# A four-layer graph network on one core: the relation layers as tiles of one relation each, edges ranked by relation on the chip

## What is computed

```
def _rgcn_layer(x, src, dst, edge_type, w_rel, root, bias):
    seg = dst * NUM_REL + edge_type
    sums = segment_sum(x[src], seg, N * NUM_REL)
    cnt = segment_sum(ones, seg, N * NUM_REL)
    mean = (sums / maximum(cnt, 1)[:, None]).reshape(N, NUM_REL, -1)
    return einsum('nrd,rdo->no', mean, w_rel) + x @ root + bias

edge_type = argmax(msg[:, 16:-16], axis=1)
h = relu(_rgcn_layer(x, src, dst, edge_type, w_rel1, root1, b1))
out = _rgcn_layer(h, src, dst, edge_type, w_rel2, root2, b2)
```

## Time and profile before

| | |
|---|---|
| median of 3 runs | 2677.25 us (2674.11 to 2680.0) |
| profiled execution, its own time | 2694.78 us |
| its span, first to last instruction | 2693.0 us |
| mean granted TensorE clock | 0.924 of 2.4 GHz |
| busy: PE, DVE, POOL, ACT | 2202.6, 2105.2, 1565.0, 1469.3 us |
| DMA | 376.34 MB, mean 140 GB/s |

### The profile page before, as it was taken

How to read it: one execution, slowest core, us unless ns; L and a number is a source line. 1 busy time by engine, 2 the same in 40 slices (tenths; PEclk the granted TensorE clock), 3 DMA queues, 4 the chain that set the end, 5 groups by cost and what they waited for, 6 DMA issues and landing times. The chain is left out here.

```text
span 2693.0 us, 53316 instructions
## 1 busy us (share of the span) xinstructions
PE 2202.6 (82%) x12829; PEld 1706.9 (63%) x12829; DVE 2105.2 (78%) x7193; ACT 1469.3 (55%) x4919; POOL 1565.0 (58%) x1653
## 2 busy tenths in 40 slices
PE   2998888888667776998776998567679999899996
PEld 2886667667555555886664898456646666555553
DVE  3667998899757776886897786588868888688886
ACT  0575555556556665665444777388844444333332
POOL 2778888888444435664886876333334444255554
PEclk9999999999878787999998989688889999899998
DMA  4666666666533435554675554344332223211221
GB/s 87 215 220 210 208 203 202 209 203 207 144 130 129 134 115 156 170 166 142 203 218 174 165 172 154 108 126 135 123 120 80 80 81 85 69 48 55 57 58 31
DMA packets 291561, 376.34 MB, mean 140 GB/s; under 512 B 59002, under 2 KB 142896, under 8 KB 291258
## 3 DMA queue, kind: packets, MB, share of 16 engines
q1 hardware_dynamic: 265658, 321.84, 37.6%
q0 software_dynamic: 25600, 51.09, 7.4%
HBM read 167.38 MB, written 206.80 MB: 139 GB/s over the span
## 5 line engine op out<-in xcount | busy, mean ns | idle before, releaser
L1808 PE MATMUL phase_p_w<-phase_w_rel,phase_rowsT 128*128 128x512 f32 (+1 forms) x1200 | 511.1, 528 | 10.3 <-ACT phase_rowsT L1861 10.2
L1889 DVE SCALAR_TENSOR_TENSOR phase_added<-phase_p_w,relation,phase_added 128x128 f32<-128x128 f32 x1200 | 349.9, 340 | 22.9 <-PE phase_p_w L1808 21.2
L1084 PE MATMUL phase_p_sum<-phase_whole,phase_link 128*128 128x128 f32 (+2 forms) x792 | 199.6, 338 | 146.7 <-ACT phase_whole L1201 65.3
L324 ACT ACTIVATE phase_sq<-phase_y 128x512 f32<-128x512 f32 x294 | 186.2, 634 | 229.9 <-POOL phase_y L457 178.9
L773 POOL DMA_INDIRECT phase_rows<-X,src_row x200 | 191.4, 957 | 202.0 <-PE phase_p_T L1816 168.0
L384 PE MATMUL phase_p_h<-W2c,phase_g 128*128 128x128 f32 x1568 | 231.5, 310 | 86.6 <-DVE phase_h L439 71.9
L384 PEld LDWEIGHTS phase_p_h<-W2c,phase_g 128*128 128x128 f32 x1568 | 220.3, 224 | 93.7 <-issue 77.1
L773 POOL DMA_INDIRECT phase_rows<-H,src_row x200 | 192.7, 963 | 135.0 <-PE phase_p_T L1816 108.8
L1152 POOL TENSOR_TENSOR phase_message<-R,scores 128x128 f32<-128x128 f32 x200 | 92.6, 464 | 284.3 <-PE phase_p_sum L1084 282.0
L1084 PEld LDWEIGHTS phase_p_sum<-phase_whole,phase_link 128*128 128x128 f32 x792 | 135.1, 213 | 188.2 <-ACT phase_whole L1201 87.8
L1808 PEld LDWEIGHTS phase_p_w<-phase_w_rel,phase_rowsT 128*128 128x128 f32 x1200 | 189.6, 193 | 86.6 <-issue 41.1
(11 more groups left out here) (254 smaller groups left out, 6876.6 us busy)
## 6 DMA issues: line engine op xcount, KB each, us to landing
H<-phase_h SPq DMA_DIRECT2D x196, 256.0 KB, 2.8
X<-phase_x SPq DMA_DIRECT2D x196, 256.0 KB, 2.3
phase_same<-same_keys SPq DMA_DIRECT2D x175, 256.0 KB
phase_xT<-in_x_columns SPq DMA_DIRECT2D x98, 256.0 KB, 4.0
Z<-phase_x SPq DMA_DIRECT2D x98, 256.0 KB
phase_x<-X SPq DMA_DIRECT2D x98, 256.0 KB
out<-phase_o SPq DMA_DIRECT2D x98, 256.0 KB
H<-R SPq DMA_DIRECT2D x50, 256.0 KB, 2.4
```

Source lines behind the costliest of these rows:

```text
L324: act.activation(self.buf(dst, g)[:, :, :], self.buf(src, g)[:, :, :], ACT.Square).then_inc(self.S[dst], 1)
L1084: last = nc.tensor.matmul(p[:, 0:width], loads.link(t), whole[1 - v][:, 0:width], start=False, stop=True)
L1808: nc.tensor.matmul(p_w[(PARTS * (t % UNROLL) + n) % BANKS][:, 0:b - a, :], rowsT[v][:, :], w[:, a:b, :], start=True, stop=True).then_inc(s ...
L1889: nc.vector.scalar_tensor_tensor(out=added[v][r % 2][:, :], in0=p_w[(PARTS * (t % UNROLL) + n) % BANKS][:, r % RG, :], scalar=plane(D["rel ...
```

## The change

An edge's rows are multiplied by the weight of its own relation alone. For that, edges are ranked by relation in `prepare_edges`: counts by relation and tile from two products with a triangle and with ones, a running sum over tiles, and starts of relations rounded up to whole tiles of 128. That gives each edge a place in a second order of 108 tiles (`REL_TILES`), each with edges of one relation only, and each tile the column of its weight (`weight_column`).

- `attention_rows` writes, by 100 indirect scatters of one number a slot, the source row of each edge to its place (`sorted_rows` in HBM); `hidden_rows` loads the list.
- A new stage `relation_products` gathers source rows in the relation order (ring of 12), transposes, multiplies each tile by one weight of 128 columns, and stores the products to HBM. Transposes, products and copies go in groups of four tiles. TensorE reads the column of the weight from SBUF into a register for each tile.
- `relation_rows` gathers the products in the order of targets (`sorted_read`), and sums. The factor 1/count (`share`, one reduction at the end of `gat_messages`) is multiplied into the table of equal keys, four tiles at a time. The root product stays in SBUF (`D["R"]`), so `x_root` goes. The bias is added to `Y` in `relation_products`, four tiles at a time, by DVE in place of POOL.
- Dense work is dealt anew: 70, 75, 55, 32 and 25 slots beside `hidden_rows`, `output_rows`, `gat_messages`, `weights_of_edges` and `gat_rows`, 70 beside the first `relation_products`, and the rest, 82, beside the first `relation_rows`. The output layer's two stages have none.

```diff
+REL_TILES = 108
+HIDDEN_SLOTS, OUTPUT_SLOTS, GAT_SLOTS, GAT_ROWS_SLOTS, PRODUCT_SLOTS = 70, 75, 55, 25, 70
...
 def prepare_edges(nc, io, W, D):
...
+                for n in range(2):
+                    part = D["relation"][:, n * T // 2:(n + 1) * T // 2, :].rearrange("p t r -> p (t r)")
+                    nc.tensor.matmul(p_here[:, n, 0:HALF], upto[:, :], part, start=True, stop=True)
+                    nc.tensor.matmul(p_tile[:, n, 0:HALF], ones[:, :], part, start=True, stop=True).then_inc(s["counted"], 1)
...
+                chained(nc.vector.tensor_tensor(D["relation"][:, :, :], D["relation"][:, :, :], wide(valid), ALU.mult))
+                nc.vector.memset(keep[:, :, :], 1.0).then_inc(s["relation_full"], 1)
...
+                chained(nc.vector.tensor_tensor_scan(flat(through), flat(keep), flat(in_tile), 0.0, ALU.mult, ALU.add))
...
+                chained(nc.vector.tensor_tensor(score[:, :, :], score[:, :, :], D["relation"][:, :, :], ALU.mult))
+                chained(nc.vector.tensor_reduce(place[:, :], score[:, :, :], AX.X, ALU.add))
+                chained(nc.vector.tensor_copy(D["sorted_read"][:, :], place[:, :]))
...
+                chained(nc.vector.tensor_tensor(D["sorted_write"][:, :], place[:, :], off[:, :], ALU.add))
...
+                chained(nc.vector.tensor_scalar(D["weight_column"][:, :], tile_f[:, :], float(RELATIONS - 1), float(F), ALU.min, ALU.mult))
...
 def attention_rows(nc, io, W, D, beside):
...
                         weighted(pool, nc, D, message, HEADS, s, t)
+                        moves.free(pool, t)
+                        pool.indirect_dma_start(out=io["sorted_rows"], out_offset=bass.IndirectOffsetOnAxis(ap=column(D["sorted_write"], t), axis=0),
+                                                in_=column(D["src_row"], t), in_offset=None, bounds_check=REL_TILES * F - 1,
+                                                oob_is_err=False).then_inc(moves.sem(t), 16)
...
 def hidden_rows(nc, io, W, D, beside):
...
-    places = beside.take(STEPS, 105)
+    places = beside.take(STEPS, HIDDEN_SLOTS)
...
+                sp.dma_start(D["sorted_rows"][:, :], io["sorted_rows"].rearrange("(p j) a -> p (j a)", p=F)).then_inc(s["sorted_loaded"], 16)
...
 def output_rows(nc, io, W, D, beside):
...
-    places = beside.take(STEPS, 105)
+    places = beside.take(STEPS, OUTPUT_SLOTS)
...
 def gat_messages(nc, io, W, D, beside):
...
-    places = beside.take(STEPS, 105)
+    places = beside.take(STEPS, GAT_SLOTS)
...
+                nc.vector.tensor_reduce(D["share"][:, :], D["relation"][:, :, :], AX.X, ALU.add).then_inc(s["twice"], 1)
...
 def gat_rows(nc, io, W, D, beside):
...
-    places = beside.rest(STEPS)
+    places = beside.take(STEPS, GAT_ROWS_SLOTS)
...
-                        sp.dma_start(io["x_root"][:, a:t + 1, :], D["R"][:, a:t + 1, :]).then_inc(s["root_stored"], 16)
...
+def relation_products(nc, io, W, D, table, w_rel, beside, count, hidden):
+    RING_ = 12
+    GROUPS_ = REL_TILES // UNROLL
+    STEPS = REL_TILES + 14
+    places = beside.take(STEPS, count)
     with Phase(nc) as m:
+        rows_ = [m.sb(f"rows{u}", [F, F]) for u in range(RING_)]
+        rowsT = [m.sb(f"rowsT{u}", [F, UNROLL, F]) for u in range(2)]
+        product = [m.sb(f"product{u}", [F, UNROLL, F]) for u in range(3)]
+        w = m.sb("w_rel", [F, RELATIONS * F])
+        p_T, p_product = ([m.pb(f"{n}{u}", [F, UNROLL, F]) for u in range(2)] for n in ("p_T", "p_product"))
+        landed = [m.sem(f"row_landed{u}") for u in range(RING_)]
+        stored = [m.sem(f"product_stored{u}") for u in range(3)]
+        s = m.named("w_loaded transposed rowsT_full multiplied product_full biased")
+        def group(k, lag):
+            g, r = divmod(k - lag, UNROLL)
+            return g if r == 0 and 0 <= g < GROUPS_ else None
+        with nc.Block() as block:
+            @block.sync
+            def _(sp):
+                sp.dma_start(w[:, :].rearrange("p (r f) -> p r f", r=RELATIONS), w_rel.rearrange("r p f -> p r f")).then_inc(s["w_loaded"], 16)
+                def step(k):
+                    if (g := group(k, 12)) is not None:
+                        sp.wait_ge(s["product_full"], g + 1)
+                        sp.dma_start(io["products"][g * UNROLL * F:(g + 1) * UNROLL * F, :].rearrange("(t p) f -> p t f", p=F),
+                                     product[g % 3][:, :, :]).then_inc(stored[g % 3], 16)
+                over_all_tiles(step, places, lambda i: beside.dense.sp(sp, i))
+                for u in range(3):
+                    sp.wait_ge(stored[u], 16 * len(range(u, GROUPS_, 3)))
+            @block.gpsimd
+            def _(pool):
+                def step(k):
+                    if k < REL_TILES:
+                        wait(pool, s["transposed"], (k - RING_) // UNROLL + 1)
+                        pool.indirect_dma_start(out=rows_[k % RING_][:, :], out_offset=None, in_=table,
+                                                in_offset=bass.IndirectOffsetOnAxis(ap=column(D["sorted_rows"], k), axis=0)).then_inc(landed[k % RING_], 16)
+                over_all_tiles(step, places, lambda i: beside.dense.pool(pool, i))
+            @block.tensor
+            def _(pe):
+                def step(k):
+                    if (g := group(k, 10)) is not None:
+                        if g == 0:
+                            pe.wait_ge(s["w_loaded"], 16)
+                        columns = [pe.value_load(D["weight_column"][0:1, g * UNROLL + u:g * UNROLL + u + 1], min_val=0, max_val=(RELATIONS - 1) * F)
+                                   for u in range(UNROLL)]
+                        pe.wait_ge(s["rowsT_full"], g + 1)
+                        wait(pe, s["product_full"], g - 1)
+                        for u in range(UNROLL):
+                            last = nc.tensor.matmul(p_product[g % 2][:, u, :], rowsT[g % 2][:, u, :], w[:, bass.ds(columns[u], F)], start=True, stop=True)
+                        last.then_inc(s["multiplied"], 1)
+                    if (g := group(k, 7)) is not None:
+                        wait(pe, s["rowsT_full"], g - 1)
+                        for u in range(UNROLL):
+                            j = g * UNROLL + u
+                            pe.wait_ge(landed[j % RING_], 16 * (j // RING_ + 1))
+                            last = nc.tensor.transpose(p_T[g % 2][:, u, :], rows_[j % RING_][:, :], W["ident"][:, :])
+                        last.then_inc(s["transposed"], 1)
+                over_all_tiles(step, places, lambda i: beside.dense.pe(pe, i))
+            @block.scalar
+            def _(act):
+                def step(k):
+                    if (g := group(k, 8)) is not None:
+                        act.wait_ge(s["transposed"], g + 1)
+                        wait(act, s["multiplied"], g - 1)
+                        act.copy(rowsT[g % 2][:, :, :], p_T[g % 2][:, :, :]).then_inc(s["rowsT_full"], 1)
+                over_all_tiles(step, places, lambda i: beside.dense.act(act, i))
+            @block.vector
+            def _(dve):
+                def step(k):
+                    if (g := group(k, 11)) is not None:
+                        dve.wait_ge(s["multiplied"], g + 1)
+                        if g >= 3:
+                            dve.wait_ge(stored[g % 3], 16 * (g // 3))
+                        nc.vector.tensor_copy(product[g % 3][:, :, :], p_product[g % 2][:, :, :]).then_inc(s["product_full"], 1)
+                    if hidden and k % UNROLL == 2 and k // UNROLL < PASSES:
+                        a = k // UNROLL * UNROLL
+                        y = D["Y"][:, a:a + UNROLL, :]
+                        nc.vector.tensor_tensor(y, y, over_tiles(W["b4c"]), ALU.add).then_inc(s["biased"], 1)
+                over_all_tiles(step, places, lambda i: beside.dense.dve(dve, i))
+def relation_rows(nc, io, W, D, beside, hidden):
...
+    places = beside.rest(STEPS)
...
+                        gather_tile(pool, io["products"], column(D["sorted_read"], t), rows_, gathered, s["summed"], t)
+                    if not hidden and (t := at(k, 15)) is not None:
+                        pool.wait_ge(s["normal_full"], t + 1)
+                        written.free(pool, t)
...
+                    if (t := at(k, 4)) is not None:
+                        gathered.landed(pe, t)
+                        pe.wait_ge(s["scaled"], t // UNROLL + 1)
+                        sum_to_here(pe, nc, p_sum, loads, rows_[t % GATHERS][:, :], whole, F, s, t)
...
+                    if (t := at(k, 2)) is not None and t % UNROLL == 0:
+                        n = t // UNROLL % LOADS
+                        loads.ready(dve, t)
+                        same = loads.same_[n][:, :, :]
+                        nc.vector.tensor_tensor(same, same, D["share"][:, t:t + UNROLL].unsqueeze(2).to_broadcast([F, UNROLL, F]), ALU.mult).then_inc(s["scaled"], 1)
...
+                            pre = plane(D["R"], t, 0, F)
```

(10 more changed lines are left out.)

257 lines of the change are left out of this document (110 added, 147 removed).

## The result

The changed kernel takes 2771.72 us (median of 4 runs, 2769.18 to 2774.72) against 2678.62 (4 runs): a ratio of 1.034, interval 1.030 to 1.038. It is **slower by 93 us**. The forecast had the side and the range right, but 33 us where 93 came.

The account below looks back on a forecast made before the run. Full TensorE bound the old relation stages, POOL's gather queue would pace the new: relation stages +95, moved dense groups -98, ranks +22, scatters +15, net +34, giving 2710 us after scaling to the timed median; range 2635 to 2810.

Parts of the forecast that it names:

- Bound of the new stages: Four new relation stages: POOL's gathers, 1.26 us each, set the pace; 189, 190, 152 and 272 us, 803 against 708.
- New: relation_rows, hidden: Hidden layer's relation_rows: gathers 126 us, dense groups beside them 37, start and tail 27, sum 190 us.
- Ranks +22: prepare_edges: ranking edges on the chip, with nothing beside it, adds 22 us of DVE operations and a wait for four products.
- Scatters +15: attention_rows: 100 scatters of row numbers lie mostly in POOL's idle time and add 15 us, between 0 and 114.
- Rival 3: attention_rows: the scatters stretch the stage by 45 us instead of 15, total 2740; chance 0.1.
- gat_messages -30, weights +5: gat_messages, taken as POOL-bound like output_rows, gives back 30 us with 12.5 groups fewer; weights stage grows 5 with two more.
- hidden_rows -24: hidden_rows, TensorE-bound: 8.75 dense groups fewer at 2.6 us each give back 23 us, listed as -24 by stage.
- gat_rows -30 and output_rows -19: Fewer dense groups: gat_rows gives back 30 us (17 to 52, ACT falling to 157 busy), POOL-bound output_rows 19.
- Register loads hidden: Relation products: TensorE's weight-column loads, 108 a stage, taken at 0.46 us each, stay hidden under four gathers (5.04 us).
- 1.9 us a load, 2910: Relation products: register loads at the landing time of a 64 KB load, total some 2910 us, left outside the range.
- Scaling by 0.65%: Whole kernel: the profiled 2694.78 us became 2729; the timed median is 0.65% less, so the forecast became 2710.
- Rival 2: Old stages: each of 38 moved dense groups gives back 4.6 us, 175 instead of 98, total 2634; chance 0.2.

Follow-up runs that it names:

- e4: Changed kernel with ACT copying the transposed rows (hT) at the head of its step in the hidden layer's relation_rows: 2753.28 us, ratio 1.023.
- e9: Changed kernel with the hT copy at the head of ACT's step and dense groups dealt as before the change: 2722.28 us, ratio 1.017.
- e6: Changed kernel with four more useless transposes for each tile of gat_messages, 400 in all: 2781.05 us, ratio 1.035.
- e12: Changed kernel with inner (mid scaled by a column) of hidden_rows on ACT instead of DVE: 2772.22 us, ratio 1.038.

## Why the prediction was right in side and short in size

- **Bound of the new stages: right.** POOL's gathers pace three of the four: products 191.6 and 151.1 us against 189 and 152, output rows 278.2 against 272, gathers 1.25 us apart as in the earlier trace rows. The 6 us too many in the last stage are POOL's own: a scatter took 1.07 us on average where 1.00 was taken, a gather 0.98 where 0.96, 9 us over 100 tiles, less some of the start and tail. Why they are longer was not tested (scatters took 1.01 before).
- **"New: relation_rows, hidden", 190: wrong by 20.** The step that failed is "DVE needs 25 scalings ..., less than half of the stage": it asked whether an engine was full, and none was. Two in-order queues with one PSUM bank between them made a loop of 1.73 us a tile beside no dense group. e4 opened it, 192.6 us. The terms below it were wrong too, start and tail 27 (14 to 15) and a group 1.8 (2.6), so that the 190 would have come out by luck.
- **Ranks +22: near** (25.7 to the second trace, 22.2 to the first; the front of the kernel differs by 3.5 us between two traces of one kernel). prepare_edges alone grew by 26, from 43.4 to 69.7 us at its end; the wait for the four products took 6.45 where 3 to 4 were taken.
- **Scatters +15: too high.** 100 of them made POOL 102 us busier and the stage 1.0 longer. Rival 3 falls.
- **gat_messages -30, weights +5: wrong by 29.** The failed words are "taken as bound by it too": TensorE was busy 194.03 of 204.97 us, POOL 158.62. What came in place of a saving was the same stage at 0.80 of the clock instead of 0.97; that more work on TensorE brings the clock back is shown (e6), how many us the clock ate is estimated (31). The prediction looked at the clock only in the new stages, not where TensorE lost work.
- **hidden_rows -24: too high by 15.** TensorE's share of a group, 2.6 us, was charged in full, and the stage gave 1.0: TensorE's busy time fell by 19 us and its idle time rose by 11. The cause is not settled.
- **gat_rows -30 and output_rows -19: near**, 36.7 and 17. In gat_rows ACT fell to 169 us busy, not to 157, and DVE to 183.
- **Register loads hidden: right**, 0.51 us against 0.46 taken, with less to spare than it said: the granted clock of the output products was 0.59, and a group at the low level just fills the time of four gathers. (The price that the text gives at 1.9 us a load, 2910, comes to 2928 by its own terms; nothing rests on it.)
- **Scaling by 0.65%: right in effect.** The first trace's 17 us were its own and had to go: 34 on the median of 2677 is 2711. But its row of gat_messages, 12.5 us too long with TensorE at 0.92 of the clock, was read as the stage's usual state.
- **Rival 2** had in common with the forecast that moving groups gains. It gained nothing: 54 us out of the old stages, 66 into the new, and 3 between the medians. A group gave back 1.4 us on average in the old stages, not 4.6.

The change in one sum, all from runs: sorting in the hidden layer breaks even (products and rows, bare, 153 + 183 = 336 us against 341), in the output layer it costs 62, the ranks cost 22 to 26, and moving the dense groups costs 12 in the traces, 3 in the medians. With the loop open the bare hidden pair takes 154 + 140 = 294 us (e9), 47 less than before: there the sorted form pays.

## What to carry to other kernels

Before a stage is costed by its fullest engine, look for loops between in-order queues: which operation stands in a queue behind one that waits for the very engine that waits for it. Where work is taken from a stage with a busy TensorE, its granted clock has to be read along, since a stage can hand its saving back as a lower clock. And price what is moved in both places with one run of the old placement in the new kernel: that run alone showed that 38 groups had moved for nothing, and where they were cheap.

## What the runs showed of the hardware

- 400 useless transposes in gat_messages cost 4 us and raised TensorE's granted clock from 0.80 to 0.95; with the same work as after, the stage was between 185.0 and 209.0 us long at 0.85 to 0.74.
- A DVE operation from SBUF to SBUF can be held while POOL works. With 100 scatters added in attention_rows, the scaling of the normalized rows went from 329 to 552 ns on average and the addition of the mean value from 300 to 514, 44 us in these two. All 60 of them that took over 1.4 times the shortest end within 0.2 us of the end of a POOL instruction. It is seldom the scatter itself: 13 scalings end with one, 4.6 us in all, and no addition; the rest, 46 us, end with POOL's dense operations and messages. Beside nothing but a gather, `inner` in hidden_rows was held 22 times in 65, by at most 0.24 us, and `Y + b2c` in e12 never in 64, though 26 of these ran across a gather's end. The product that makes the mean value has 12 long ones before and 15 after (360 and 337 ns on average); the statistics have none (281 and 283, longest 302). The rows of after:

```profile
L1209 DVE TENSOR_SCALAR Y<-Y,phase_norm_moments_kept,phase_norm_inverse 128x128 f32<-128x128 f32 x100 | 55.1, 552 | 0.0
L1313 DVE TENSOR_TENSOR Y<-Y,phase_mean_value 128x128 f32<-128x128 f32 x100 | 51.4, 514 | 0.0
```

The Trainium skill (SBUF — State Buffer, SBUF: two separate sides) describes an exclusive lock on a port pair that DVE and GpSimd share, held for a whole instruction. The ends that fall together agree with it.

- An indirect gather of 128 rows takes POOL 1.25 us from start to start where nothing holds it, whether the rows come from node tables or from products written the stage before (e9).
